# Edge rows, six walks, dense rows and the last hop in one part in place of four

## The chip, the cores and the metric

The kernel runs on one core of a Trainium2 chip. The metric is the device time of one execution in microseconds, from the core's own records; lower is better. The core has five engines that run side by side and wait for one another through semaphores: TensorE (PE, matrix products and transposes), VectorE (DVE), ScalarE (ACT), GpSimd (POOL, here the issuer of indirect gathers and scatters) and SyncE (SP, here the issuer of plain DMAs). Each engine executes its own instructions in order.

## The reference

Four graph layers act on 50000 nodes with 128 features and 12500 edges, sorted by destination. Each one adds to x what it makes of h = max(layernorm(x), 0):

```
x = x + gcn3(h)              # three weighted graph convolutions and a linear map
x = x + gin(h, edge_attr)    # mean over messages; W1, batch norm, relu, W2, batch norm, relu
x = x + walk6(h)             # six steps: h = h + relu(mean(h[src] into dst) @ Wh.T + bh)
x = x + gcn2(h)              # tanh(gcn(h, W1) + b1), then a second convolution's product W2
```

Only nodes that are the destination of an edge get anything from neighbours. The kernel computes the others, the great majority, as dense rows without a graph: for them the walks are a constant addition (relu of a bias, six times), and the last layer is two products with a tanh between them.

## The kernel before

Rows lie in groups of 512 (four tiles of 128 rows). There are DG = 98 dense groups (49 pairs), RG = 25 groups of "edge" rows (E: one row for the source of each edge) and 25 of "self" rows (S: one for the end of each run of edges with one destination). The edge list has NT = 98 tiles of 128, handled as 14 iterations of 4 + 3 tiles (halves b = 0 and 1). The parts are closed blocks with a barrier between them:

- First two layers' graph work and dense rows (0 to 1317 us), then the batch norms (1317 to 1917). The latter write y2_tab, turned group by group (`HI`, lines 1421 to 1438 for its loads and stores). The change touches only how self rows are loaded there.
- **Edge and self rows** (class `Late`, tag c, lines 1623 to 1726): 25 pairs. A pair loads y2 and x1, ScalarE applies the second batch norm and relu (L1594), PE turns it (L1601), DVE adds x1 (L1608), takes the moments (L206, L215), ScalarE the root (L221) and the normed rows (L252). Normed rows go to step_tab, what the third layer will be added to goes to x2_tab, with the constant r6 added for edge rows (L1720). The next load of x1 waits for this addition, since X1 has one buffer per half.
- **Walks and dense rows** (tag d, lines 1733 to 1962). Six walks of 14 iterations. In an iteration POOL gathers rows of step_tab (L287), PE turns them (L330 to L335), DVE sums along the edges by a scan (L344), PE multiplies by Wh (L355), DVE scales and adds the bias (L364) and updates RS (L1918), and SP stores RS to the other step_tab (L1889). POOL begins a walk only when all stores of the walk before have landed. Each gather buffer G[b] is used again once PE has turned it. `beside` orders the dense pairs between them by hand: one lone pair more than walks at the start, one lone pair before each walk, and one pair beside each two iterations ("a paired slot"): 7 lone pairs and 42 paired ones. In a pair DVE adds the rows three times: x2 (L1608), x3 (L1770), and the output rows of the pair before (L1796), whose products (L1818, L1825, L1831, L1833) PE does in the same slot, "late".
- **Third input** (tag p, lines 1974 to 2081): x2_tab and the walked rows are added for E and S rows, normed, and stored to last_tab (the fourth layer's input) and x3_s.
- **Last hop** (tag f, lines 2087 to 2183): 14 iterations: gather from last_tab, add RS (L315), turn, scan, product, affine, tanh (L2173), turn (L2157), copy (L2177), product (L2162), addition (L2141), and a scatter of the output rows by POOL (L2113), which stands between gathers: iteration i+1 is gathered before i is scattered.

## Time and profile before

| | |
|---|---|
| median of 3 runs | 3704.01 us (3700.06 to 3708.16) |
| the profiled execution | 3697.86 us |
| its span, first to last instruction | 3695.9 us |
| busy: PE, PE weight loads, DVE | 69%, 45%, 62% |
| busy: ACT, POOL | 54%, 40% |
| DMA | 549.48 MB, mean 149 GB/s |

The profile is one execution. Busy shares are averages over all parts. PEclk is the clock granted to TensorE as a share of 2.4 GHz (0.5 is 1.2 GHz). "Idle before" tells how long an engine stood before an instruction and what ended it.

### The profile page before, as it was taken

What the parts mean: (1) busy time and instruction counts of PE and PEld (TensorE: products, weight loads), DVE (VectorE), ACT (ScalarE), POOL (GpSimd) and SP (SyncE); (2) the same over time, 40 slices, a digit from 0 to 9 for tenths busy, and PEclk for the clock granted to TensorE, in tenths of its full rate; (3) what the DMA queues carried; (4) which work ended last, traced back from release to release, by engine and by line L of the source; (5) the groups of instructions that cost most, each with busy time, mean ns of one, the idle gap of its engine ahead of it and who ended that gap; (6) DMA issues with size and microseconds to landing.
All of it is one profiled execution on the core that took longest, in us unless ns stands there. A gap on an engine that the chain in (4) does not pass through costs nothing. (4 is left out here: it accounts for less than half of the span.)

```text
span 3695.9 us, 53510 instructions
## 1 busy us (share of the span) xinstructions
PE 2567.6 (69%) x11598; PEld 1680.0 (45%) x11598; DVE 2284.9 (62%) x8624; ACT 2000.0 (54%) x4312; POOL 1492.2 (40%) x1590
## 2 busy tenths in 40 slices
PE   5787677776566689999961116788888888840453
PEld 2455445544445544444431104555656565620343
DVE  6656777777775523333344327978888788878332
ACT  2788778565455535555544436665565656556110
POOL 6676762543325500000000003554555464635676
PEclk8999888897778889999985557888988898875666
DMA  4676554444545433333337664544444444349222
GB/s 102 197 203 192 146 153 147 141 140 144 146 136 160 144 109 135 135 136 136 136 135 234 215 206 139 160 151 144 145 146 152 141 150 130 118 145 294 68 73 62
DMA packets 548708, 549.48 MB, mean 149 GB/s; under 512 B 59898, under 2 KB 390891, under 8 KB 548400
## 3 DMA queue, kind: packets, MB, share of 16 engines
q1 hardware_dynamic: 490962, 441.21, 37.9%
q0 software_dynamic: 53264, 105.38, 10.3%
q10 hardware_dynamic: 4316, 1.13, 0.1%
q8 instruction: 51, 0.84, 0.1%
q14 instruction: 115, 0.93, 0.1%
HBM read 272.64 MB, written 279.69 MB: 149 GB/s over the span
## 5 line engine op out<-in xcount | busy, mean ns | idle before, releaser
L287 POOL DMA_INDIRECT h_G<-step_tab,row_i x588 | 565.5, 962 | 501.4 <-PE h_P L332 182.7
L287 POOL DMA_INDIRECT h_G<-msg_tab,row_i x294 | 283.0, 963 | 430.9 <-DVE h_M L307 181.5
L344 DVE TENSOR_TENSOR_SCAN h_T<-keep,h_T,h_P 128x384 f32<-128x384 f32 (+3 forms) x308 | 351.2, 1140 | 58.1 <-PE h_P L332 31.4
L808 PE MATMUL a_PA<-a_H,w 128*128 128x512 f32 x504 | 276.7, 680 | 94.3 <-ACT a_H L964 91.9
L252 ACT ACTIVATE d_NR<-d_X,d_ln_nm,d_ln_rs 128x128 f32<-128x128 f32 x784 | 311.7, 481 | 49.7 <-DVE d_ln_nm L235 49.7
L1513 DVE TENSOR_SCALAR b_Y<-b_BP,col 128x512 f32<-128x512 f32 x148 | 109.9, 742 | 354.1 <-PE b_BP L1467 354.1
L335 PE MATMUL h_P<-ident,h_M 128*128 128x128 f32 x490 | 100.5, 356 | 316.2 <-DVE h_M L315 249.6
L1467 PE MATMUL b_BP<-b_Z,w 128*128 128x512 f32 x592 | 266.3, 592 | 0.0
L1495 ACT ACTIVATE b_Z<-b_BQ,bn 128x512 f32<-128x512 f32 x148 | 115.0, 777 | 256.4 <-PE b_BQ L1459 256.0
L335 PEld LDWEIGHTS h_P<-ident,h_M 128*128 128x128 f32 x490 | 78.3, 186 | 356.1 <-DVE h_M L315 155.8
L1555 POOL TENSOR_TENSOR b_d<-b_d,neghalf 128x1 f32<-128x1 f32 x1 | 0.6, 568 | 592.1 <-DVE b_d L1546 592.1
L973 ACT ACTIVATE a_H<-a_PA,col 128x512 f32<-128x512 f32 x252 | 162.9, 669 | 87.9 <-PE a_PA L808 87.2
L252 ACT ACTIVATE a_HI<-a_X,a_ln_nm,a_ln_rs 128x128 f32<-128x128 f32 x490 | 200.9, 484 | 12.7 <-DVE a_ln_nm L235 12.7
L1601 PE MATMUL c_PT<-ident,c_ZT 128*128 128x128 f32 x200 | 49.6, 427 | 221.9 <-ACT c_ZT L1594 221.9
L1183 DVE TENSOR_TENSOR a_X<-a_XR,a_P 128x512 f32<-128x512 f32 x126 | 83.2, 670 | 186.9 <-PE a_P L830 185.2
L364 DVE SCALAR_TENSOR_TENSOR h_Z<-h_P,inv_cnt,rbh 128x128 f32<-128x128 f32 x588 | 162.2, 341 | 50.6 <-PE h_P L355 49.9
L808 PEld LDWEIGHTS a_PA<-a_H,w 128*128 128x128 f32 x504 | 97.0, 215 | 199.5 <-ACT a_H L964 121.6
L221 ACT ACTIVATE d_ln_sd<-d_ln_mv,lneps 128x8 f32<-128x8 f32 x98 | 29.2, 298 | 277.0 <-DVE d_ln_mv L215 277.0
L830 PE MATMUL a_P<-w3l,a_H 128*128 128x128 f32 x980 | 171.0, 327 | 0.0
L355 PEld LDWEIGHTS h_P<-wht,h_T 128*128 128x128 f32 x1176 | 147.1, 194 | 48.4 <-issue 37.7
L332 PE MATMUL h_P<-ident,h_G 128*128 128x128 f32 x980 | 167.0, 317 | 0.0
L252 ACT ACTIVATE a_NR<-a_XR,a_ln_nm,a_ln_rs 128x128 f32<-128x128 f32 x392 | 155.8, 484 | 12.7 <-DVE a_ln_nm L235 12.6
(343 smaller groups left out, 6549.2 us busy)
## 6 DMA issues: line engine op xcount, KB each, us to landing
b_HI<-hin_tab SPq DMA_DIRECT2D x148, 256.0 KB, 2.8
y_tab<-b_Y SPq DMA_DIRECT2D x148, 256.0 KB, 2.0
x_tab<-a_X SPq DMA_DIRECT2D x112, 256.0 KB
hin_tab<-a_HI SPq DMA_DIRECT2D x112, 256.0 KB
d_Y<-y_tab SPq DMA_DIRECT2D x98, 256.0 KB, 3.3
d_X<-x_tab SPq DMA_DIRECT2D x98, 256.0 KB
a_XR<-in_x SPq DMA_DIRECT2D x97, 256.0 KB, 4.1
out_rows<-d_O SPq DMA_DIRECT2D x97, 256.0 KB
```

The lines of the kernel that those rows point to most:

```text
L252: last = nc.scalar.activation(normed[:, k, :], rows[:, k, :], AF.Relu, scale=self.rs[:, c:c + 1], bias=self.nm[:, c:c + 1])
L287: pool.indirect_dma_start(out=G[b][:, j, :], out_offset=None, in_=self.table[:, :], in_offset=bass.IndirectOffsetOnAxis(ap=row_i[:, t + j: ...
L332: last = nc.tensor.matmul(PH[b][:, j * P:(j + 1) * P], rows[b][:, j, :], ident[:, :], start=False, stop=(j == nt - 1))
L335: last = nc.tensor.transpose(PH[b][:, j * P:(j + 1) * P], rows[b][:, j, :], ident[:, :])
L344: nc.vector.tensor_tensor_scan(T[b][:, 0:nt * P], keep[:, bass.ds(t * P, nt * P)], PH[b][:, 0:nt * P], T[1 - b][:, w - 1:w], ALU.mult, ALU ...
L355: last = nc.tensor.matmul(out_t, sums, self.W[:, :], start=True, stop=True)
L364: last = nc.vector.scalar_tensor_tensor(Z[b][:, j, :], PH[b][:, j * P:(j + 1) * P], self.scale[:, bass.ds(t + j, 1)], self.bias[:, :], ALU ...
L808: nc.tensor.matmul(PA[b][:, 0:nt * P], w[:, :], h[b][:, 0:nt, :].rearrange("p t d -> p (t d)"), start=True, stop=True).then_inc(done, 1)
L830: last = nc.tensor.matmul(P3[b][:, k * P:(k + 1) * P], H2[b][:, k, :], w3l[:, :], start=False, stop=(k == nt - 1))
L973: nc.scalar.activation(dst_h[b][:, 0:nt, :], PA[b][:, 0:nt * P], AF.Relu, bias=col[:, c:c + 1]).then_inc(done, 1)
L1467: last = nc.tensor.matmul(BP[b][:, :], w12[:, c, :], ZT[c][b][:, :], start=(c == 0), stop=(c == 1))
L1495: nc.scalar.activation(ZT[c][b][:, :], (BQ, BQ2)[c][b][:, :], AF.Relu, bias=bn1[:, 2 + c:3 + c], scale=bn1[:, c:c + 1]).then_inc(b_z[c], 1)
```

## The change

One block takes the place of the four behind the batch norms. Its slots are laid out in a list, and all loops are written out (no hardware loops).

- 25 slots of one pair each: self rows first (12 pairs and a half), then edge rows. Y, X1, X2, NR have two buffers per half. Edge rows get their third input at once: PE sums r6, X2 and the normed rows in PSUM, the second norm follows one slot later and goes to last_tab. Self rows stay in SBUF (XS), in place of x2_tab and x3_s.
- Walks: a lone dense pair ahead of walks 0, 1 and 2 alone. Seven paired slots in walks 0 to 4, six in walk 5, whose last slot has two iterations and no pair. Gathers alternate between the tiles G and M.
- In walk 5, each iteration also adds RS to XS, takes moments (`end_stats`), root (`end_rstd`) and norm (`end_norm`), stored to last_tab.
- Last hop: 14 slots of one iteration, with the last five dense pairs beside iterations 1, 3, 5, 7 and 9. All gathers come ahead of all scatters; the scatters wait for the dense stores.
- Output rows of a pair: PE adds X2 by a matmul with the identity, ScalarE copies the rows out (`rows_out`); L1796 goes.
- Batch-norm part: self groups are loaded with rows of one tile per partition (512 bytes each). free_d is bf16, and each iteration loads its share of it (`FR`).

```diff
-    free_d = dram("free_d", (1, EP))
+    free_d = dram("free_d", (1, EP), BF16)
-    x2_tab = dram("x2_tab", (2 * RR, D))
-    x3_s = dram("x3_s", (EP, D))
...
+                    if ends[b]:
+                        rows = hin_tab[bass.ds((2 * j + b) * GR, GR), :].rearrange("(k p) d -> p k d", p=P)
+                    else:
+                        rows = group_rows(hin_tab, 2 * j + b)
...
+    slots, left = [Slot3(j, ()) for j in range(D0)], collections.deque(range(D0, NJ))
+    ALONE3, LAST_PAIRS, TAIL_PAIRS = STEPS - 3, IT // 2 - 1, 5
+    for w in range(STEPS):
+        if w < ALONE3:
+            slots.append(Slot3(left.popleft(), ()))
+        for i in range(0, IT, 2):
+            with_pair = w < STEPS - 1 or i // 2 < LAST_PAIRS
+            slots.append(Slot3(left.popleft() if with_pair else None, (w * IT + i, w * IT + i + 1)))
+    for i in range(IT):
+        slots.append(Slot3(left.popleft() if i % 2 and left else None, (STEPS * IT + i,)))
...
+        @block.gpsimd
+        def _(pool):
+            def gather(i):
+                table = step_tab[i // IT % 2] if i < F0 else last_tab
+                for b in range(2):
+                    n, t, nt = hop_at(i, b)
+                    after(pool, wk_turn, n - 3)
...
+            for w in range(STEPS + 1):
+                for b in range(2):
+                    if 0 < w < STEPS:
+                        pool.wait_ge(wk_st[b], 16 * IT * w)
+                    if w == STEPS:
+                        pool.wait_ge(l_st[b], 16 * IT)
+                        pool.wait_ge(o_st[b], o_stores(D0, b))
+                for i in range(IT):
+                    gather(w * IT + i)
+            for b in range(2):
+                pool.wait_ge(o_st[b], o_stores(NJ, b))
+            for i in range(IT):
+                scatter(i)
...
+            def x3(j):
+                for b in range(2):
+                    if full(j, b):
+                        r = j % 2
+                        pe.wait_ge(ln1.normed, 2 * j + b + 1)
+                        nc.tensor.matmul(XB[r][b][:, :], ones3[:, :], split_r6[:, :], start=True, stop=False)
+                        if not is_d(j):
+                            nc.tensor.matmul(XB[r][b][:, :], ident[:, :], X2[r][b][:, :, :].rearrange("p t d -> p (t d)"), start=False, stop=False)
+                        nc.tensor.matmul(XB[r][b][:, :], ident[:, :], NR[r][b][:, :, :].rearrange("p t d -> p (t d)"), start=False,
+                                         stop=True).then_inc(x3_sum, 1)
...
+            def rows(j):
+                for b in range(2):
+                    n = 2 * (j - D0) + b
+                    pe.wait_ge(tanh_set, n + 1)
+                    pc_user[b] = (tanh_set, n + 1)
+                    nc.tensor.matmul(XB[j % 2][b][:, :], ident[:, :], X2[j % 2][b][:, :, :].rearrange("p t d -> p (t d)"), start=True, stop=False)
+                    nc.tensor.matmul(XB[j % 2][b][:, :], ones3[:, :], split_out[:, :], start=False, stop=False)
+                    for k in range(4):
+                        last = nc.tensor.matmul(XB[j % 2][b][:, k * P:(k + 1) * P], HT[b][:, k, :], w32[:, :], start=False, stop=(k == 3))
+                    last.then_inc(p2_set, 1)
...
+            for sl in slots:                                  # PE's order
+                j, its = sl.pair, sl.its
+                if j is not None and MIX < j <= D0:
+                    x3(j - 1)
+                if j is not None:
+                    turn(j)
+                for i in its[:1]:
+                    hop_turn(i)
+                if late is not None:
+                    turn2(late)
+                    prod(late)
+                for i in its[:1]:
+                    hop_prod(i)
+                if late is not None:
+                    rows(late)
+                for i in its[:1]:
+                    if i >= F0:
+                        end_turn(i - F0)
+                for i in its[1:]:
+                    hop_turn(i)
+                if j is not None and is_d(j):
+                    x3(j)
+                for i in its[:1]:
+                    if i >= F0:
+                        end_prod(i - F0)
+                for i in its[1:]:
+                    hop_prod(i)
...
+            for sl in slots:                                  # ScalarE's order
+                if late is not None:
+                    h(late)
+                if j is not None:
+                    ln1.act_std(act, j)
+                if j is not None and MIX < j <= D0:
+                    ln2.act_std(act, j - 1 - MIX)
+                for i in its[:1]:
+                    if LASTW < i < F0:
+                        pn.act_std(act, i - LASTW - 1)
+                        end_norm(i - LASTW - 1)
...
+                if late is not None:
+                    tanh(late)
+                for i in its[:1]:
+                    if i >= F0:
+                        end_tanh(i - F0)
+                if j is not None:
+                    z(j + 1)
+                    norm1(j)
+                    if j < D0 and j > MIX:
+                        norm2(j - 1)
...
+                if late is not None:
+                    rows_out(late)
...
+            for sl in slots:                                  # VectorE's order
...
+                if j is not None:
+                    x2(j)
+                    if MIX < j <= D0:
+                        stats2(j - 1)
+                for i in its[:1]:
+                    sums(i)
+                if j is not None:
+                    ln1.dve_rstd(dve, j)
+                    if MIX < j <= D0:
+                        rstd2(j - 1)
+                for i in its[:1]:
+                    if LASTW < i < F0:
+                        end_rstd(i - LASTW - 1)
+                    for b in range(2):
+                        affine(i, b)
+                    if i < F0:
+                        update(i)
+                    if LASTW <= i < F0:
+                        end_stats(i - LASTW)
+                for i in its[1:]:
+                    sums(i)
+                if j is not None and is_d(j):
+                    stats2(j)
+                for i in its[1:]:
+                    affine(i, 0)
+                    if i > LASTW:
+                        end_rstd(i - LASTW - 1)
+                if j is not None and is_d(j):
+                    rstd2(j)
+                for i in its[1:]:
+                    affine(i, 1)
+                    update(i)
+                    if i >= LASTW:
+                        end_stats(i - LASTW)
```

## Rows read from the trace of the kernel before

**Rows 1.** Windows by part: length, busy time (instructions) of PE, PEld, DVE, ACT, POOL, PEclk, DMA share, GB/s

```profile
1920.00:2191.00 271.00, 49.63 (x200) 38.94 (x200) 110.98 (x525) 120.16 (x275) 0.00 (x0) 0.50 0.65 216
2191.00:3285.00 1094.00, 892.70 (x4550) 613.26 (x4550) 864.34 (x2983) 647.44 (x1274) 566.15 (x589) 0.86 0.46 142
...
3424.00:3696.00 272.00, 126.91 (x588) 103.56 (x588) 92.67 (x182) 32.22 (x57) 192.52 (x196) 0.64 0.22 66
```

**Rows 2.** Windows: seven paired slots of walk 0, of walk 3, one lone pair

```profile
2256.00:2401.00 145.00, 114.12 (x596) 79.83 (x597) 132.74 (x450) 94.63 (x187) 84.81 (x90) 0.84 0.51 158
...
2767.00:2924.00 157.00, 134.68 (x712) 94.85 (x712) 133.10 (x448) 93.71 (x186) 86.37 (x90) 0.90 0.47 147
...
2751.00:2767.00 16.00, 14.76 (x60) 8.34 (x60) 9.33 (x43) 11.84 (x24) 7.84 (x9) 0.80 0.49 156
```

**Rows 3.** Timeline of a paired slot, walk 3: start, length, engine, line, [idle before]

```profile
2780.45 1.28 DVE L344 TENSOR_TENSOR_SCAN h_T<-keep,h_T,h_P 128x512 f32<-128x512 f32 x1 [0.90 <-PE h_P L332]
...
2795.43 1.01 DVE L344 TENSOR_TENSOR_SCAN h_T<-keep,h_T,h_P 128x384 f32<-128x384 f32 x1 [0.21 <-DVE h_T L344]
...
2797.37 0.39 PE L1831 MATMUL d_PC<-split_out,ones 3*128 3x512 bf16 x1
...
2799.65 1.32 DVE L1796 TENSOR_TENSOR d_O<-d_X,d_PC 128x512 f32<-128x512 f32 x2
...
2800.18 0.38 PE L330 MATMUL h_P<-freed,split_msg 9*128 x1
...
2801.99 1.28 DVE L344 TENSOR_TENSOR_SCAN h_T<-keep,h_T,h_P 128x512 f32<-128x512 f32 x1 [1.02 <-PE h_P L332]
```

**Rows 4.** Timeline, the same slot: identity matmul of a dense half, two passes

```profile
2803.03 1.12 PE L1810 MATMUL d_PC<-d_NR,ident 128*128 128x512 f32 x2
```

**Rows 5.** Timeline: POOL behind a walk, and the first gathers of the last hop

```profile
2754.81 0.95 POOL L287 DMA_INDIRECT h_G<-step_tab,row_i  x1 [16.79 <-DMA step_tab<-RS]
...
3426.43 1.02 POOL L287 DMA_INDIRECT h_G<-last_tab,row_i  x1 [5.62 <-POOLq L72]
...
3432.80 0.73 DVE L315 TENSOR_TENSOR h_M<-h_G,RS 128x512 f32<-128x512 f32 x1 [18.50 <-DMA h_G<-last_tab,row_i]
...
3436.57 0.60 DVE L315 TENSOR_TENSOR h_M<-h_G,RS 128x384 f32<-128x384 f32 x1 [3.04 <-DMA h_G<-last_tab,row_i]
```

**Rows 6.** Timeline: an edge pair, and the first input pass of the dense rows

```profile
1941.60 1.64 DVE L206 BATCH_NORM_STATS2 c_ln_st<-c_X 128x6 f32<-128x128 f32 x8
1941.78 3.18 ACT L252 ACTIVATE c_R<-c_X2r,c_ln_nm,c_ln_rs 128x128 f32<-128x128 f32 x8 [4.93 <-DVE c_ln_nm L235]
1943.41 0.64 DVE L215 BATCH_NORM_AGGREGATE c_ln_mv<-c_ln_st 128x2 f32<-128x6 f32 x8 [0.17 <-DVE c_ln_st L206]
1944.87 1.51 ACT L1594 ACTIVATE c_ZT<-c_Y,bn 128x512 f32<-128x512 f32 x2
1945.80 1.96 PE L1601 MATMUL c_PT<-ident,c_ZT 128*128 128x128 f32 x8 [7.75 <-ACT c_ZT L1594]
1949.05 0.69 DVE L1608 TENSOR_TENSOR c_X2r<-c_X,c_PT 128x512 f32<-128x512 f32 x1 [3.82 <-DMA c_X<-x_tab]
...
2221.48 0.81 ACT L1594 ACTIVATE d_ZT<-d_Y,bn 128x512 f32<-128x512 f32 x1 [33.71 <-DMA d_Y<-y_tab]
```

**Rows 7.** Timeline: PE behind the pause between walks 2 and 3

```profile
2751.20 1.12 PE L1818 MATMUL d_PC<-ident,d_NR 128*128 128x128 f32 x4 [3.79 <-ACT d_NR L252]
...
2753.65 3.62 PE L1825 MATMUL d_PC<-d_HT,w 128*128 128x512 f32 x4
```

**Rows 8.** Groups by line, 2000 to 3700: count | busy us, mean ns | idle before

```profile
L2113 POOL DMA_INDIRECT out_rows<-f_OR,end_i x98 | 97.1, 990 | 37.8 <-issue 29.3 <-DVE f_OR L2141 8.5
...
L1855 ACT ACT_TABLE_LOAD x49 | 62.9, 1283 | 0.9
```

**Rows 9.** Timeline: one iteration of the last hop, messages and output addition

```profile
3447.84 1.18 DVE L315 TENSOR_TENSOR h_M<-h_G,RS 128x512 f32<-128x512 f32 x2
...
3457.76 1.15 DVE L2141 TENSOR_TENSOR f_OR<-f_XR,f_P 128x512 f32<-128x512 f32 x2 [2.68 <-PE f_P L2162]
```

More of the change, by code:

```diff
@@ L1433, in _ @@
             load(1)
-            with sp.Fori(0, BPAIRS - 2) as j:
+            FIRST = (DG + RG) // 2
+            with sp.Fori(0, FIRST - 2) as j:
                 load(j + 2)
+                store(j)
+            load(FIRST, (False, True))
+            store(FIRST - 2)
+            with sp.Fori(FIRST - 1, BPAIRS - 2) as j:
+                load(j + 2, (True, True))
                 store(j)
@@ new lines, in group, with width, full, no2 @@
+    def group(j, b):
+        if j < MIX:
+            return 2 * j + b
+        if j == MIX:
+            return RG - 1
+        return 2 * (j - MIX - 1) + b if j < D0 else 2 * (j - D0) + b
+    def width(j, b):
+        return NT - 4 * (RG - 1) if j == MIX and b == 1 else 4
+    def full(j, b):
+        return kind(j, b) != "S"
+    def no2(j, b):
+        return max(j - MIX, 0) - (1 if b == 1 and j > MIX else 0)
+    def is_d(j):
+        return j >= D0
+    Slot3 = collections.namedtuple("Slot3", "pair its")
@@ new lines, in build, with hop_at @@
+    assert not left and slots[-1].pair is None and slots[-2].pair is None
+    LASTW, F0 = (STEPS - 1) * IT, STEPS * IT
+    def hop_at(i, b):
+        return 2 * i + b, first_tile(i % IT, b), SUB[b]
+    XS = sb(ctx, "XS", [P, NT, D])
+    FR = [sb(ctx, f"l_FR{u}", [3 * (STEPS - 1), sum(SUB) * P], BF16) for u in range(2)]
+    ring = lambda n: [[sb(ctx, f"l_{n}{r}{b}", [P, 4, D]) for b in range(2)] for r in range(2)]
+    Y, X1, X2, NR = ring("Y"), ring("X1"), ring("X2"), ring("NR")
+    HT, O = ([sb(ctx, f"l_{n}{b}", [P, 4, D]) for b in range(2)] for n in ("HT", "O"))
@@ L1655, in build, with r_stores, o_stores, rows2 @@
+    def r_stores(j, b):
+        return sum(32 for p in range(j) if p % 2 == j % 2 and kind(p, b) == "E")
+    def o_stores(j, b):
+        return 16 * no2(j, b)
+    def rows2(j, b):
+        return X2[j % 2][b] if full(j, b) else _Rows(XS, 4 * group(j, b))
     with nc.Block() as block:
@@ L1727, in build @@
-    end(ctx)
-    lctx = phase()
-    dl = Late(lctx, "d", True)
-    freed = sb(lctx, "freed", [3 * (STEPS - 1), EP], BF16)
-    rs_in, freed_in = sem("rs_in"), sem("freed_in")
-    HALF = IT // 2
-    def first(j):
-        return isinstance(j, int) and j == 0
-    def final(j):
-        return isinstance(j, int) and j == PAIRS - 1
-    def dl_load_next(sp, j):
-        if not (isinstance(j, int) and j == PAIRS - 1):
-            for b in range(2):
-                sp.wait_ge(dl.x2, 2 * j + b + 1)
-                dl.load(sp, j + 1, 0, b)
@@ L1827, in dl_pe_rows @@
-    def dl_pe_rows(pe, j):
-        for b in range(2):
-            q = 2 * j + b
-            pe.wait_ge(dl.tanh, q + 1)
-            nc.tensor.matmul(dl.PC[b][:, :], ones3[:, :], split_out[:, :], start=True, stop=False)
-            for k in range(4):
-                last = nc.tensor.matmul(dl.PC[b][:, k * P:(k + 1) * P], dl.HT[b][:, k, :], w32[:, :], start=False, stop=(k == 3))
-            last.then_inc(dl.p2, 1)
-    def dl_pe_end(pe, j):
-        dl_pe_turn2(pe, j)
-        dl_pe_prod(pe, j)
-        dl_pe_rows(pe, j)
@@ L2124, in _ @@
+            for b in range(2):
+                pool.wait_ge(o_st[b], o_stores(NJ, b))
+            for i in range(IT):
                 scatter(i)
@@ L2166, in _ @@
[L2166 to L2178 removed]
+                    q, r, n = 2 * j + b, j % 2, width(j, b)
@@ new lines, in affine @@
+            def affine(i, b):
+                n, t, nt = hop_at(i, b)
+                scale, bias = (inv_cnt, rbh) if i < F0 else (dinvu, rb31)
+                dve.wait_ge(wk_prod, n + 1)
+                if i <= F0:
+                    after(dve, wk_out, n - 1)
+                else:
+                    dve.wait_ge(f_prod, n - 2 * F0 - 1)
+                for k in range(nt):
+                    last = nc.vector.scalar_tensor_tensor(Z[b][:, k, :], PH[b][:, k * P:(k + 1) * P], scale[:, t + k:t + k + 1],
+                                                          bias[:, :], ALU.mult, ALU.add)
+                last.then_inc(wk_z, 1)
```

876 lines of the change are left out of this document (378 added, 498 removed).

## The prediction

> **What bounds the kernel now.** I read the busy times stage by stage first [rows 1]. The part behind the batch norms takes 1779 of the 3696 us: edge and self rows (271), walks with dense pairs (1094), the edge rows' third input (the 139 between 3285 and 3424), last hop (272). Then came the walks apart [rows 2]. Walk 3 has seven paired slots in 157 us, 22.4 each; the other walks from 1 to 5 span up to 159, so I use 22.6. Walk 0 gives 145/7 = 20.7, and a lone dense pair 16.0. Last came one paired slot in order of time [rows 3], because busy shares do not say which order matters: DVE is busy 85% of the walk windows, PE 86%.
>
> In that slot the loop is plain. DVE starts the scan of the second iteration at 2780.45 and is then occupied, with gaps of some tenths, until the scan of the next first iteration ends (2795.43 + 1.01 = 2796.44): 16.0 us. PE then finishes the product, starts the late pair's output rows at 2797.37, holds them until 2800.18, turns the gathered rows, and DVE's next scan starts at 2801.99, 5.55 us after the last. Together 21.54 us. The output addition of the late pair (L1796, 1.32 us) is done by 2800.97, and the scan behind it still waits 1.02 us for PE. So PE's work between two scans counts in full, and that DVE addition counts for nothing.
>
> **The change part by part.** I count profiled microseconds after minus before. The profiled run took 3697.86, 1.96 above its span, 6.15 below the median 3704.01; I add the sum of differences to the median.
>
> *Paired slots of walks 0 to 4.* The addition X2 + product moves from DVE into PSUM as a 128x512 fp32 matmul by the identity, once per half, and a ScalarE copy takes the rows out. DVE's 1.3 us was in the gap: gain 0. A 128x512 fp32 matmul is two passes, 1.12 us with its tail at full clock [rows 4]; I take 0.95 each, 1.9 per pair, between the two scans. The ring of two gather buffers removes PE's waits for gathers (0.9 us in most slots, ahead of the DVE-set point), which pays back part of any slow stretch but not of the loop above. So 21.54 + 1.9 = 23.45 for an undisturbed slot; I take 23.5 for the 28 slots of walks 1 to 4, against 22.6: +25. In walk 0, DVE's addition ended only as PE did, so a little comes back: 22.2 against 20.6, seven slots: +11. Bounds per slot: -1.3 (DVE is the bound and its addition is saved whole) to +1.9.
>
> *Lone pairs.* Seven before, three after. One costs 16.0 now [rows 2]; after, the same 1.9 longer, and the first also carries the last edge pair's second norm: 20 + 2 x 17.8 = 56 against 112: -56. But a lone pair covers the pause between walks: POOL gathers again only at 2754.81 [rows 5], 3.6 us after DVE has begun the lone pair [rows 2]. Where no lone pair stands, the first scans wait for that: four tiles need 3432.80 - 3426.43 = 6.4 us, all seven 10.1 [rows 5], so the second scan can start near 2754.8 + 10.1 + 1.3 = 2766.2, and end at 2767.2 instead of 2757.6 as DVE's order alone would have it. +9.6 at the walks 3, 4 and 5: +29.
>
> *Edge and self pairs (25 slots).* Before, each waits for its load, which is single buffered: DVE idles 3.8 us for it [rows 6], slots average 10.8. The rings of two take that wait away. Next late for a self pair: ScalarE's input pass 1.5, four transposes of its second half 1.1 (of 1.96 for eight), the addition 0.69, stats and aggregation 1.82 + 0.65, root 0.3: 6.1 us [rows 6]; DMA moves 1.5 MB in it, so I take 6.6. Twelve and the start: 5 + 79 us. An edge pair now gets its second norm here. The loop goes through all engines: first norm of half b0 1.6, on PE a small bf16 pass and four fp32 passes of 512 columns for each half (2.0 us at full clock, 3.9 at half) and the transposes (1.0 or 2.0), addition 0.7, two rounds of stats 2.5 each, roots and shifts 0.7, input pass 1.5, so that with the handovers I count 14.0 us with PE at full clock, 18.9 at half. PE idles over half of that. After 3.79 us of idleness its clock is at the lower level: four passes of 512 columns take 3.62 us [rows 7], 0.9 each, where two take 1.12 with their tail at the full one [rows 4]. I take 17 (PE slow in the first 6 us of its burst, as in that lone slot). 13 x 17 = 221. Together 305 us from the barrier to the first dense addition. Before it is 271 + 33 (ScalarE stands idle 33.71 us until 2221.48 behind the barrier, [rows 6]) = 306. So -1, with 13 x -3 to 13 x +2 around it.
>
> The Trainium skill, "TensorE: Matmul & The Clock Gate", section "HAM oscillation", says that a loop in which PE waits between bursts pays the cold clock once per burst. The trace agrees: 3.62 us behind the pause [rows 7]. By that rule alone, with every burst short, edge slots would be 18.9 and the term +24.
>
> *Third input.* x2_tab, x3_s and the stage that reads them go: -139. Its work for the self rows moves into walk 5: per iteration two additions, seven stats, seven aggregations (3.3 us on DVE) and a masked root (0.65), and seven norms on ScalarE (2.8 of the 3.18 for eight, [rows 6]).
>
> *Walk 5.* For a slot's first iteration DVE's 3.3 us fall into the gap before the second scan. ScalarE's do not: its norm of the previous iteration stands ahead of the tanh of the late pair, waits for DVE's masked root (7.15 us into the slot), and ends at 9.95; tanh's table 1.28 [rows 8] and b0 0.65 let PE begin the late rows at 11.9 instead of 7. PE has then idled 4 us and is slow for 6: rows and turn take 9 instead of 6.1; scan at 21. The second iteration's 3.3 + 0.65 on DVE are bare. Sum 21 + scan, third sum, stats, affine, root, update, end stats 14.5 = 35.5 us (32.5 with no slow clock). Six of these, one slot without a pair 27, and 7.3 us until its norms are stored and POOL gathers: 247. Before: 7 x 22.6 + 12 of drain (the two products behind the last update) = 170. +77.
>
> *Last hop.* Before POOL alternates 98 gathers and 98 scatters, 1.26 us apart ([rows 5], three more tiles in 3.8) and 1.29 (0.99 and 0.30 of issue, [rows 8]): 250 of 272 us. After, all gathers come first, hidden behind dense pairs, and the scatters last: 98 x 1.29 = 126 us in which no other engine has work. They start when the 14th gather is out, and that needs the turn of iteration 11. Iterations without a pair take 11.1 us from messages to output ([rows 9], 3447.84 to 3458.91), and are no longer overlapped. Per pair, two slots: one with the pair 21 (full clock) to 24, the next with its late rows 15 to 20; I take 40 for both. 7 + 3 (first gathers) + 11.6 + 5 x 40 + 3.5 + 8.8 + 126.4 + 2.5 = 363: +91. Bounds 36 and 44: +71 to +111.
>
> The self rows' loads of 512 bytes in the batch-norm part lie under a PE that runs without a pause; nought. The bf16 free flags save a small copy; nought.
>
> Sum: 25 + 11 - 56 + 29 - 1 - 139 + 77 + 91 = +37. 3704 + 37 = **3741 us**.
>
> **The rivals.**
> 1. *The clock stays up* (faster). PE has more work per slot and loses its waits for gathers; if the granted clock stays at the full level in edge slots, walk 5 and last hop: 13 x -3, 6 x -3, 5 x -4, 28 x -0.3, and the self rows near 6.1 (-6): -91, so 37 - 91 = -54: 3650. For it: the walks hold 0.90. Against: 0.64 in the last hop and 0.50 with the edge rows, where bursts are short [rows 1, 2]. It decides the sign once 37 of these 91 us come back. 17%.
> 2. *DVE is the bound of paired slots* (faster). Then each loses 1.3 instead of gaining 0.9 to 1.6: 28 x -2.2, 7 x -2.9, lone ones 3 x -2: -88: 3653. For it: DVE's 85%. Against: the 1.02 us wait in [rows 3]. 6%.
> 3. *Slow stretches everywhere* (slower than forecast). PE at the low clock behind each wait for the affine rows: paired slots 24.2 (+20), edge 18.9 (+25), last hop 44 a pair (+20), walk 5 37 (+9): 3815. 22%.
> 4. *It nets out*: the terms of +77 and +91 are each some 17 too high: 3707. 13%.
>
> **How the numbers follow.** Forecast 42%, the rivals as given. About 0.2%, 7 us, is what a measurement tells from no change. Faster: rivals 1 and 2, 0.23, and little of 4: 0.25. Same: most of 4, 0.12. Slower: 0.63. The forecast's own range is 3715 to 3770; with the others cut at one in ten on either side 3665 to 3805.
>
> **What would show it.** Scan to scan in a paired slot of walks 1 to 4: 23.5 us with the identity matmuls right behind the tanh and DVE idle some 3 us before the second scan; under 22 means rival 2. Edge slots 17 us apart and a granted clock between the levels; 14 means rival 1. DVE idle some 8 us at the start of walks 3, 4 and 5. In walk 5 ScalarE's norm of RS ahead of each tanh, slots of 35. At the end 126 us of scatters alone, starting some 235 us after the first gather of the last hop. If compute of the last hop ends early and POOL starts scattering before that, or the slots of walk 5 stay under 30, the prediction fails there.

## The result, and the profile after

The change makes the kernel slightly slower: median 3711.11 us (3701.69 to 3721.35, 20 runs) against 3697.44 us (3688.70 to 3708.16, 20 runs) for the kernel before, ratio 1.0037, 95% interval 1.0029 to 1.0046. Two later jobs gave 1.0036 and 1.0032. That is +14 us where +37 was forecast. The profiled execution spans 3708.4 us, 12.5 more than before.

Windows of the kernel after, columns as in [rows 1]: twelve self slots, twelve edge slots, walk 0, the second lone pair, walks 1 and 3, four paired slots of walk 5, and the last hop ahead of its scatters and from them on.

```profile
1921.70:1995.70 74.00, 23.62 (x98) 18.83 (x97) 47.42 (x241) 54.87 (x126) 0.00 (x0) 0.50 0.84 254
2006.60:2212.40 205.80, 97.84 (x218) 38.70 (x217) 75.97 (x457) 92.87 (x236) 0.00 (x0) 0.69 0.42 150
2230.70:2383.40 152.70, 126.34 (x623) 80.16 (x623) 123.69 (x435) 101.61 (x201) 81.68 (x86) 0.90 0.47 146
2383.40:2400.90 17.50, 15.40 (x64) 8.56 (x64) 7.83 (x41) 12.44 (x24) 10.74 (x12) 0.90 0.59 183
2400.90:2563.80 162.90, 142.59 (x740) 94.09 (x740) 124.52 (x435) 101.53 (x201) 83.51 (x87) 0.95 0.44 138
2744.30:2919.60 175.30, 146.59 (x756) 98.23 (x756) 124.56 (x436) 99.79 (x197) 94.25 (x98) 0.91 0.45 138
3134.70:3271.90 137.20, 99.80 (x432) 61.42 (x432) 98.67 (x401) 80.90 (x177) 58.36 (x60) 0.81 0.33 103
...
3338.00:3571.50 233.50, 172.19 (x766) 115.64 (x767) 115.18 (x355) 108.61 (x196) 93.24 (x99) 0.76 0.17 52
3571.50:3708.40 136.90, 15.66 (x92) 11.86 (x91) 13.73 (x27) 4.33 (x8) 95.88 (x98) 0.57 0.12 38
```

The seven slots of walk 3 take 175.3 us where before they and the lone pair ahead of them took 157 + 16 [rows 2]. In the last 136.9 us POOL issues the 98 scatters (95.9 us busy); the other engines end their last iterations in the first 23 us of it (PE 15.7 us busy, DVE 13.7, ScalarE 4.3) and then stand idle. The steady slot of walks 1 to 4, timeline of DVE and PE (as [rows 3]):

```profile
2688.37 2.38 DVE L2118 TENSOR_TENSOR_SCAN h_T<-keep,h_T,h_P 128x512 f32<-128x512 bf16 x2 [3.71 <-PE h_P L1865]
...
2701.95 2.35 DVE L2118 TENSOR_TENSOR_SCAN h_T<-keep,h_T,h_P 128x512 f32<-128x512 bf16 x2
...
2711.28 2.39 DVE L2118 TENSOR_TENSOR_SCAN h_T<-keep,h_T,h_P 128x512 f32<-128x512 bf16 x2 [3.78 <-PE h_P L1865]
...
2705.14 1.02 PE L1844 MATMUL l_XB<-l_X,ident 128*128 128x512 f32 x2
...
2709.76 0.38 PE L1863 MATMUL h_P<-l_FR,split_msg 6*128 6x512 bf16 x1
```

Scan to scan is 22.91 us, and DVE stands 3.78 us for PE before the second scan (some 3 forecast). PE's output rows now last 4.62 us (2705.14 to 2709.76) where they took 2.81 [rows 3]: the identity passes cost 1.81.

From boundary to boundary of the two traces, after minus before, forecast in brackets: self and edge pairs from the barrier to the first dense addition -11.2 (-1); lone pairs 18.3 + 17.5 + 17.4 = 53.2 against 112.9, -59.7 (-56); walk 0 +8.2 (+11); walks 1 to 4 with two of the boundaries +41.8 (+25 +19); walk 5 with its boundary, to POOL's first gather of the last hop, +74.1 (+77 +10); third input -141.4 (-139); last hop +100.7 (+91). Sum +12.5, the difference of the spans.

### The profile page after: what moved, and what is told of

It is laid out like the page before. It is cut to its first block and busy times, and to the rows that moved or that the text cites. A ratio compares the mean times of both kernels' runs of the same rounds, so it can differ in the third digit from the quotient of the medians.

```text
span 3708.4 us, 48145 instructions
## 1 busy us (share of the span) xinstructions
PE 2722.3 (73%) x11947; PEld 1703.4 (46%) x11947; DVE 2178.1 (59%) x8443; ACT 2055.6 (55%) x4419; POOL 1429.5 (39%) x1505
## 5 line engine op out<-in xcount | busy, mean ns | idle before, releaser
L1762 POOL DMA_INDIRECT h_G<-step_tab,row_i x294 | 289.5, 985 | 542.5 <-DMA step_tab<-l_NR 300.1
L1762 POOL DMA_INDIRECT h_M<-step_tab,row_i x294 | 280.0, 953 | 274.3 <-PE h_P L1865 170.1
L2118 DVE TENSOR_TENSOR_SCAN h_T<-keep,h_T,h_P 128x512 f32<-128x512 bf16 x196 | 223.4, 1140 | 213.0 <-PE h_P L1865 180.5
L219 ACT ACTIVATE l_ln_sd<-l_ln_mv,lneps 128x8 f32<-128x8 f32 (+1 forms) x136 | 40.9, 301 | 479.5 <-DVE l_ln_mv L2090 313.0
L250 ACT ACTIVATE l_NR<-l_X,l_ln_nm,l_ln_rs 128x128 f32<-128x128 f32 x492 | 195.2, 482 | 0.0
L1181 DVE TENSOR_TENSOR a_X<-a_XR,a_P 128x512 f32<-128x512 f32 x126 | 83.3, 671 | 190.1 <-PE a_P L828 188.4
L1963 ACT ACTIVATE l_NR<-l_X,l_ln_nm,l_ln_rs 128x128 f32<-128x128 f32 x392 | 156.0, 480 | 39.5 <-DVE l_ln_nm L2101 39.5
L2130 DVE SCALAR_TENSOR_TENSOR h_Z<-h_P,inv_cnt,rbh 128x128 f32<-128x128 f32 x588 | 162.2, 342 | 17.5 <-PE h_P L1876 17.4
L1876 PE MATMUL h_P<-wht,h_T 128*128 128x128 f32 x1176 | 154.6, 281 | 11.3 <-DVE h_T L2118 11.2
L1821 PE MATMUL l_XB<-l_NR,ident 128*128 128x512 f32 x246 | 158.5, 731 | 0.0
```

The lines of the kernel that those rows point to most:

```text
L250: last = nc.scalar.activation(normed[:, k, :], rows[:, k, :], AF.Relu, scale=self.rs[:, c:c + 1], bias=self.nm[:, c:c + 1])
L1762: pool.indirect_dma_start(out=GR_[i % 2][b][:, k, :], out_offset=None, in_=table[:, :], in_offset=bass.IndirectOffsetOnAxis(ap=row_i[:, t ...
L1821: nc.tensor.matmul(XB[r][b][:, :], ident[:, :], NR[r][b][:, :, :].rearrange("p t d -> p (t d)"), start=False, stop=True).then_inc(x3_sum, 1)
L1876: last = nc.tensor.matmul(PH[b][:, k * P:(k + 1) * P], T[b][:, k * P:(k + 1) * P], (wht if i < F0 else w31)[:, :], start=True, stop=True)
L1963: last = nc.scalar.activation(to[:, k, :], rows, AF.Relu, scale=ln2.rs[:, c:c + 1], bias=ln2.nm[:, c:c + 1])
L2118: nc.vector.tensor_tensor_scan(T[b][:, 0:nt * P], keep[:, t * P:(t + nt) * P], PH[b][:, 0:nt * P], T[1 - b][:, w - 1:w], ALU.mult, ALU.add ...
```

## The experiments

Eighteen runs were made, in five jobs: twelve kernels, four of them twice, and the changed kernel itself twice. In the second and the fourth job (e4, e8, e5, e7; c1, c4, e7b, e4b) everything took longer: the part up to the start of the new block, the same in all kernels after, ended at 2209 to 2274 us in place of 1916 to 1929, and the kernel before took 4181 and 4130 us. From these two jobs I use comparisons inside a job alone. I took their transfers for slow, and the expectations below say so, but the profiles do not bear it out. Windows of that common part, the kernel after and e7b (fourth job):

```profile
100.00:1917.00 1817.00, 1442.59 (x6066) 897.82 (x6064) 1042.74 (x4067) 1089.23 (x2424) 604.12 (x632) 0.90 0.49 147
```

```profile
100.00:2214.00 2114.00, 1521.23 (x6088) 947.84 (x6087) 1050.33 (x4104) 1095.18 (x2430) 610.97 (x638) 0.84 0.42 128
```

The DMA engines were busy as long in both (0.49 x 1817 and 0.42 x 2114 us, 890 and 888) and moved about the same bytes in a longer time. What the slow job adds are waits for which the profile names no releaser: before L1181, for example, DVE stood 204 us in such waits ("remote" 113.6, "issue" 90.0), against 1.7 in the kernel after. What held the engines there is not known. I call these two the slow jobs.

**e1: the output addition back on DVE.** PE's identity matmul goes, and DVE adds X2 from SBUF to the product in PSUM behind the first affine and update.

```diff
-  nc.tensor.matmul(XB[j % 2][b], ident, X2[j % 2][b], start=True, stop=False)
-  (ScalarE) activation(O[b], XB[j % 2][b], AF.Copy)
+  (VectorE) tensor_tensor(O[b], X2[j % 2][b], XB[j % 2][b], ALU.add)
```

> The changed kernel with one part undone: the output rows of a dense pair are added by VectorE again, behind the update of the slot's first iteration, and the identity matmul of X2 and ScalarE's copy are gone. Theory A (the prediction's: what PE does between the scan of a first iteration and the scan of the second counts in full, and VectorE's addition lies in the wait for it): a paired slot of walks 1 to 4 falls from 22.9 us by the two identity matmuls, 0.95 each, to 21.1; in walk 5 from 34.3 to some 31 (PE is at its low clock there, two passes take up to 2.1); walk 0, bound by both, 21.1 to 20.3. Over 28 + 7 + 6 slots, three lone ones and five pairs of the last hop some 75 us, 3636 by the clock of the 3711. Theory B (the slot is bound by VectorE's own work): VectorE gets 1.3 us more per slot and the slot grows to 24. Theory C (nothing in it, the cost was only ScalarE's): 22.9 stays.

Measured 3632.29 us, ratio 0.9822 (0.9805 to 0.9839), 79 below the kernel after. Steady slots are 21.18 us each (21.1 expected). DVE's timeline in one of them:

```profile
2632.80 1.42 DVE L2094 TENSOR_TENSOR l_O<-l_X,l_XB 128x512 f32<-128x512 f32 x2
2634.94 2.38 DVE L2122 TENSOR_TENSOR_SCAN h_T<-keep,h_T,h_P 128x512 f32<-128x512 bf16 x2 [0.72 <-PE h_P L1864]
```

DVE does the addition and then still waits 0.72 us for PE: it was free there, as the forecast took it to be, and PE's passes were not. 22.91 - 21.18 = 1.73 a slot, close to the 1.81 by which the passes had lengthened PE's rows. (ScalarE's copy left with them; e1 does not part the two.) This one edit is the difference between a change that costs 14 us and one that saves 63.

**e2: the late pair ahead of a walk's first gathers** on PE, in the slots where walks 3, 4 and 5 begin.

```diff
+  if early: turn2(late); prod(late)
   for i in its[:1]: hop_turn(i)
-  if late is not None: turn2(late); prod(late)
+  if late is not None and not early: turn2(late); prod(late)
```

> The changed kernel with TensorE's order changed in three slots, the first of walks 3, 4 and 5, which have no lone pair ahead of them: the late pair's transposes and first product come before the transposes of the walk's first gathered rows. Theory A (the pause costs more than predicted because TensorE, waiting for the gather, has the late pair's work queued behind it): the first slot of walks 3 and 4 falls from 37.5 to some 33, that of walk 5 from 40.4 to 36, and the kernel by 12 to 15 us to 3697. Theory B (the extra comes from gathers or stores landing later than predicted): no change of the three slots beyond 0.5 us.

Measured 3700.63 us, 1.0019 (1.0007 to 1.0031), 10.5 below after. The start of walk 3 in the kernel after, POOL, PE and DVE:

```profile
2747.68 0.95 POOL L1762 DMA_INDIRECT h_G<-step_tab,row_i  x1 [27.70 <-DMA step_tab<-RS]
...
2753.94 0.60 PE L1863 MATMUL h_P<-l_FR,split_msg 9*128 9x512 bf16 x1 [13.49 <-DMA h_G<-step_tab,row_i]
...
2759.52 1.92 PE L1830 MATMUL l_PC<-ident,l_NR 128*128 128x128 f32 x8
2761.27 2.98 PE L1837 MATMUL l_PC<-l_HT,w 128*128 128x512 f32 x4
2764.09 1.72 PE L1876 MATMUL h_P<-wht,h_T 128*128 128x128 f32 x14
...
2771.79 2.39 DVE L2118 TENSOR_TENSOR_SCAN h_T<-keep,h_T,h_P 128x512 f32<-128x512 bf16 x2 [3.64 <-PE h_P L1865]
```

And in e2:

```profile
2742.46 3.36 PE L1837 MATMUL l_PC<-l_HT,w 128*128 128x512 f32 x4
2749.60 0.60 PE L1863 MATMUL h_P<-l_FR,split_msg 9*128 9x512 bf16 x1 [3.78 <-DMA h_G<-step_tab,row_i]
...
2755.25 3.19 PE L1876 MATMUL h_P<-wht,h_T 128*128 128x128 f32 x14
```

PE waited 13.49 us for the gather with the late pair's work queued behind it, and only then did that work (4.6 us) ahead of the first product. Moved into the wait, it brings the first slots of walks 3, 4, 5 from 37.5, 37.1, 40.4 to 34.8, 35.0, 38.9: 6.3 us, half of what was expected. The first product starts 4.5 us sooner in its slot, but then takes 3.19 us in place of 1.72. The other 4.2 us are not of the edit: in the profiled executions 1.2 lie ahead of the new block and 3.0 in the edge part (287.7 us for 290.7), which the edit leaves alone, and a second execution of the unaltered kernel (r1_after) takes 287.4 there.

**e3: ScalarE norms RS behind the late tanh.** `end_norm` of a slot's first iteration moves from ahead of `tanh(late)` to behind the pair's norms.

```diff
   pn.act_std(act, i - LASTW - 1)
-  end_norm(i - LASTW - 1)
   if late is not None: tanh(late)
   ... norm1(j) ...
+  end_norm(i - LASTW - 1)
```

> The changed kernel with ScalarE's norm of the walked rows (end_norm of a slot's first iteration, walk 5 alone) moved from ahead of the late pair's tanh to behind its own first norm of the dense pair. Theory A (that norm, with its wait for VectorE's masked root, is what makes walk 5's slots long): a slot of walk 5 falls from 34.3 by the 2.8 of the norm and 1 to 2 of wait and of TensorE's slow clock, to 29 to 31; six slots, 20 to 30 us, 3686. Theory B (VectorE's stats are the bound of these slots: its work sums to 27.5 with the gaps that remain): less than 2 us a slot, 3700 or more.

Measured 3673.28 us, 0.9942 (0.9924 to 0.9961): -38, where 20 to 30 were expected. Walk 5's slots fall from 34.3 to 26.6. One slot of it in the kernel after:

```profile
3210.24 2.80 ACT L250 ACTIVATE RS<-XS,p_ln_nm,p_ln_rs 128x128 f32<-128x128 f32 x7 [2.58 <-DVE p_ln_nm L233]
3213.06 1.28 ACT L1978 ACT_TABLE_LOAD   x1
...
3215.09 2.08 PE L1844 MATMUL l_XB<-l_X,ident 128*128 128x512 f32 x2 [4.71 <-ACT l_HT L1978]
...
3223.98 2.38 DVE L2118 TENSOR_TENSOR_SCAN h_T<-keep,h_T,h_P 128x512 f32<-128x512 bf16 x2 [7.70 <-PE h_P L1865]
```

And in e3:

```profile
3185.63 1.28 ACT L1978 ACT_TABLE_LOAD   x1
3186.92 1.26 ACT L1978 ACTIVATE l_HT<-l_PC,col 128x512 f32<-128x512 f32 x2
...
3188.35 1.02 PE L1844 MATMUL l_XB<-l_X,ident 128*128 128x512 f32 x2
...
3194.49 2.38 DVE L2120 TENSOR_TENSOR_SCAN h_T<-keep,h_T,h_P 128x512 f32<-128x512 bf16 x2 [0.26 <-PE h_P L1865]
```

The late rows on PE begin 6.9 us after the slot's start (3181.47) in place of 11.6 (3203.51), and without the pause of 4.71 us PE does them at the upper clock: an identity pair of passes takes 1.02 where it took 2.08. DVE's idle time before the second scan falls from 7.70 to 0.26, which is what the slot gains.

**e6: the kernel before with its walk loops written out**, nothing else.

```diff
-  with eng.Fori(0, HALF - 1) as k:
+  for k in range(HALF - 1):
```

> The kernel before with one edit: the hardware loops over the paired slots of the walks are written out, all else is as it was. Theory A (half a microsecond of the difference between the predicted 23.45 and the measured 22.9 us of an undisturbed slot is what loop registers and computed addresses cost at the handovers between VectorE and TensorE): slots of walks 1 to 5 fall from 22.6 on average by 0.3 to 0.5, and the kernel by 12 to 18 us, to 3682. Theory B (the 0.5 comes from something else, such as the second gather buffer): no change within 3 us.

Measured 3690.89 us, 0.9986 (0.9971 to 1.0001): not told from no change by the times, and less than the 12 to 18 us that theory A asked of the kernel. Windows of walks 1 to 4 with their lone pairs, kernel before and e6:

```profile
2416.60:3115.20 698.60, 602.73 (x3088) 415.90 (x3088) 570.75 (x1960) 423.53 (x833) 377.92 (x393) 0.88 0.47 146
```

```profile
2421.10:3110.20 689.10, 596.10 (x3088) 414.74 (x3088) 569.17 (x1962) 423.02 (x832) 375.99 (x393) 0.89 0.47 149
```

9.5 us in 28 slots, 0.3 each, from one execution of either. So of the 1.4 by which e1's slots (21.18) are shorter than those of before (22.6), loops give 0.3. That the rest comes of PE's missing waits for gathers is argued, not shown.

**e5: a busy PE in the edge slots.** Sixteen more matmuls per edge pair, into a PSUM tile that nobody reads then.

```diff
+  if MIX < j < D0:
+      for r in range(16):
+          nc.tensor.matmul(PC[r % 2][:, 0:2 * D], w31, w11, start=True, stop=True)
```

> The changed kernel with 16 more matmuls (128x256, results overwritten) on PE behind the transposes of each edge pair, in the time in which PE stands idle. It asks whether the 17.1 of an edge slot hold a share of low clock. Theory A (PE's passes at the low clock cost 3 of the 17.1, as the prediction put it): slots of about 14 to 15, granted clock near 1.0 there, 12 slots 25 to 35 less. Rival B (ScalarE and DVE round the loop set it, or the added work itself is in the way): slots within 0.5 of 17.1 or longer.

Windows of eleven edge slots, e5, and e7 as its base in the same job (its one gather buffer plays no part in edge slots):

```profile
2361.90:2528.40 166.50, 143.46 (x553) 94.69 (x552) 69.73 (x419) 86.46 (x220) 0.00 (x0) 0.95 0.48 171
```

```profile
2371.10:2558.70 187.60, 88.56 (x200) 35.03 (x199) 69.67 (x418) 86.40 (x220) 0.00 (x0) 0.70 0.43 152
```

With 353 more passes (16 matmuls of two passes in each slot) the stretch is 21 us shorter: slots of 17.06 become 14.38 (six) or 15.98 (five), and the granted clock is 0.95 in place of 0.70. The total, 4135.24 us, ratio 0.9879 (0.9840 to 0.9917), is 22 above e7's 4113.31: walks 3, 4 and 5 began with slots of 48.9, 49.0 and 52.0 us where e7's were 38.4, 37.4 and 42.9. RS's stores are not the cause, since POOL's first gather of walk 3 comes 3.4 us after the slot's start in both. In e5 DVE then stands 11.5 us before the affine rows (L2133), against 4.5, and 4.7 before a reciprocal (L230), against 1.8, for reasons that the profile does not name. So the edit's worth in a job like the first was not measured.

**e7 and e7b: one gather buffer.**

```diff
-  GR_ = [G, M]
+  GR_ = [G, G]
...
-  after(pool, wk_turn, n - 3)
+  after(pool, wk_turn, n - 1)
```

> The changed kernel with one gather buffer per half in place of two, so that a gather waits for the turn of the iteration before it. It asks what the second buffer gives back in the paired slots. Theory A: the slots of walks 1 to 4, an even 22.9 now, spread between 22 and 24.5 again and grow by 0.5 to 1 (PE waits for gathers at the head of a slot, some tenths of a us to 1.2 of waiting): total +15 to +30. Rival B (PE waits were hidden in any case): within 5.

> The changed kernel with one gather buffer per half. Theory A: slots of walks 1 to 4 grow from an even 22.9 to 23.4 or more, the size the forecast gave them; total +15 to +30 (3725 to 3740). Theory B (the second buffer hides nothing in an undisturbed slot): slots 22.9, total within 5, and the forecast's 23.5 was high for another reason: the pause around PE's section was counted too long.

4113.31 us (0.9831, 0.9796 to 0.9865) and 4056.17 us (0.9832, 0.9801 to 0.9862), both in slow jobs. Walk 1's six slots behind its first, e7b, and e4b with two buffers in the same job:

```profile
2731.30:2876.20 144.90, 128.63 (x640) 86.29 (x640) 107.72 (x373) 85.73 (x169) 73.42 (x77) 0.89 0.44 139
```

```profile
2734.50:2875.70 141.20, 126.84 (x640) 85.51 (x639) 107.75 (x374) 85.18 (x168) 66.50 (x70) 0.91 0.45 140
```

0.6 us a slot for the second buffer, in a slow job (in walk 1 both kernels place their pairs alike). In the other jobs it was not measured. Ratios near 0.983 say little of the buffer: in the slow jobs every kernel with the new block gained on the one before, and the changed kernel itself never ran in such a job (r2_after met an ordinary one).

**e4 and e4b: pairs back where they were; e8 and e8b: none in the last hop, POOL in turn.** All four also put the late pair ahead on PE where the last hop starts, as e2 does for the walks, and issue the last store of normed rows sooner.

```diff
-  ALONE3, LAST_PAIRS, TAIL_PAIRS = STEPS - 3, IT // 2 - 1, 5
+  e4: STEPS, IT // 2, 1     e8: two lone pairs ahead of walk 0, one ahead of the others, IT // 2, 0
...
   e8 only:
-  for i in range(IT): gather(F0 + i)
-  for i in range(IT): scatter(i)
+  gather(F0); gather(F0 + 1); scatter(0)
+  for i in range(1, IT): gather(F0 + i + 1) (to IT - 1); scatter(i)
```

> The changed kernel with its dense pairs placed nearly as before: a lone pair ahead of every walk (six), a pair beside all seven slots of walk 5, one pair in the last hop in place of five; nothing else differs, scatters still follow all gathers. Theory A (the terms as read from the two traces): three more lone pairs +52 (17.5 each), the first slots of walks 3 to 5 fall from 37, 37 and 40 to about 24 (-43), one more pair in walk 5 +9 (34.3 for 25.3), four pairs less in the last hop -75 (41 for two iterations with a pair, some 22 without): -57, about 3654. Rival B (pairs beside the last hop are free, since gathers and scatters by POOL bound it as they did before): the last hop stays within 15 of its 370, and the sum is about 3700 or more.

> The changed kernel with no pair in the last hop (two lone pairs ahead of walk 0, one ahead of each other walk, seven beside walk 5) and with POOL taking the gathers and scatters of the last hop in turn, as before. Theory A: the last hop takes the 270 that it took before instead of 370 (-100); four more lone pairs +70, first slots -43, walk 5 +9: -64, about 3647. Rival B (alternating makes gathers late, because one iteration now has norms and stores ahead of it): the last hop stays above 330, about 3710.

> The changed kernel with six lone pairs, seven pairs in walk 5 and one in the last hop; scatters behind all gathers. On the slow chip its last hop took 354 from the first gather, there against some 382 with five pairs. Theory A (the pairs ride in idle time, the scatters behind the gathers are what costs): last hop 330 to 350 here, 60 to 75 more than e8b's 275 and 20 to 40 less than the changed kernel's 370; total 3685 to 3705. Theory B (pairs cost 19 each beyond an iteration's own length): last hop about 295, total about 3650.

> The same placement as e8: no pair in the last hop, seven lone pairs, gathers and scatters of the last hop in turn. On the slow chip the last hop without pairs took 341 from its first gather where 270 were expected, and POOL waited 82 us for DVE's output rows. Theory A (expected first, 270 for the last hop): 64 below the changed kernel. Theory B (the last hop is longer because one iteration's work no longer overlaps the next one's; its five pairs ride in time that is idle anyhow): last hop about 340 against 370, so -30 +70 -43 +9: within 15 of the changed kernel.

e8b, in an ordinary job: 3665.24 us, 0.9921 (0.9902 to 0.9940), 44 below the changed kernel (r1_after, 3709.58, same job), expected 64; by spans 56.6. Its last hop takes 275.4 from the first gather, where the changed kernel's took 370.7: theory A. The same kernel's 341 in e8 was the slow job's. e8 was 4121.99 (0.9843, 0.9812 to 0.9874). e4 and e4b, both in slow jobs: 4119.13 (0.9836, 0.9805 to 0.9866) and 4067.39 (0.9855, 0.9819 to 0.9891). e4b's last hop took 349.7 where e7b's with five pairs took 386.7, so four pairs less are worth 37 there, 9 each; in the other slow job e4 took 354.0 against 386.2 (e7) and 402.1 (e5), so this is rough. c1 below, no pair and in turn, took 323.4 in e4b's job: 26 less. What e4 gives in an ordinary job, where 57 us were expected, was not measured.

**e9, c3, c4: two iterations overlapped in the last hop.** DVE adds and scans iteration i+1, and PE turns it, ahead of iteration i's end. c3 is e9 with e1, e3 and e2's order. c4 has one edit more:

```diff
-  gather(F0 + i + 1) ahead of scatter(i)
+  gather(F0 + i + 2) ahead of scatter(i)
```

> e8 with one thing more: in the last hop DVE adds and scans iteration i+1, and PE turns it, ahead of the tanh, turn and product of iteration i, so that two iterations overlap as they did in the kernel before. Theory B above: POOL's 196 gathers and scatters at 1.27 become the bound again, last hop 255 to 275, 70 less than e8b. Theory A (alternation alone was enough, or the time goes to something else): within 10 of e8b.

> All that gained, together: e9's placement and overlap, the output addition back on DVE (e1, -77), the norms of RS behind the affine half of the slot (e3, -38; one slot of walk 5 more has a pair now, so somewhat more), the late pair first where a walk or the last hop starts (e2; here only at the last hop, since lone pairs stand before the walks). Theory A (the gains add): -77 -42 and e9's -85 from the changed kernel's 3710: about 3505, 0.948 of before. Rival B (they share the same idle time, half of the smaller ones is lost): about 3560.

e9: 3759.28 us, 1.0174 (1.0155 to 1.0192), 94 above e8b, against both theories. c3: 3661.05 us, 0.9901 (0.9872 to 0.9930), 156 above theory A and 101 above rival B. POOL's groups in the last hop (count | busy, mean ns | idle before), e8b, e9 and c4b:

```profile
L1770 POOL DMA_INDIRECT out_rows<-XS,end_i x98 | 99.5, 1015 | 38.4 <-issue 29.3 <-DVE XS L2164 9.1
```

```profile
L1770 POOL DMA_INDIRECT out_rows<-XS,end_i x98 | 96.5, 985 | 139.8 <-DVE XS L2167 112.3 <-issue 27.5
```

```profile
L1770 POOL DMA_INDIRECT out_rows<-XS,end_i x98 | 98.5, 1005 | 29.9 <-issue 29.6 <-DVE XS L2173 0.3
```

And e9's order in time, POOL and DVE:

```profile
3419.39 0.95 POOL L1762 DMA_INDIRECT h_G<-last_tab,row_i  x1 [0.30 <-issue]
...
3421.89 0.56 DVE L2119 TENSOR_TENSOR h_G<-h_G,RS 128x384 f32<-128x384 f32 x1 [3.03 <-DMA h_G<-last_tab,row_i]
...
3427.59 0.69 DVE L2167 TENSOR_TENSOR XS<-XS,l_PC 128x512 f32<-128x512 f32 x1 [2.85 <-PE l_PC L1900]
...
3429.11 1.01 POOL L1770 DMA_INDIRECT out_rows<-XS,end_i  x1 [8.76 <-DVE XS L2167]
```

POOL gathers for i+1 and then waits to scatter i; DVE's output rows of i now stand behind its work on i+1, which waits for that very gather. So POOL idles ahead of each iteration's scatters, some 8.7 us a time, 112 us in all. I had moved the work on one queue and not asked what the other queue's order relied on.

> e8's placement and its gathers and scatters in turn, with e1 (addition on DVE), e3 (norms of RS later on ScalarE) and e2's order at the last hop; it is c3 without the overlap that lengthened e9. In c3 the last hop began at 3288 from the start; e8b's takes 275 from there. Theory A (c3's 3661 holds all of e9's error): about 3565, 0.965 of before. Theory B (the overlap was not the cause there): near 3660.

> c3_best with one change in POOL's order: two iterations are gathered before the first is scattered, and so on. In e9 POOL stood idle 112 us before scatters, because DVE's output rows of iteration i stood behind its addition for i+1, which waits for the gather that POOL issued last. Theory A (that ring of waits is what e9 lost): the last hop falls from 373 to POOL's own 196 x 1.28 = 251 and some 10 to 20 around it, about 3555, 5 to 15 below c1. Rival B (the overlapped order itself is slow, ScalarE's 213 us of waiting for PE's turns): it stays over 3600.

> The changed kernel unaltered, as the base for the three others on the same chip. The job before this one landed on a chip where the kernel before takes 4181 us, and had no such base: there the kernel with one gather buffer was at 0.983 of before. Theory A (on a chip like the first, before at 3697): 1.0037 of before, as measured. Theory B (should the chip be the slow one): 0.98 or below, since the slow chip's stores and loads cost the four old blocks with their barriers more than the one new block.

> The changed kernel unaltered. If this job finds fast transfers (before near 3697): 1.0037 of before again. If it finds slow ones (before over 4100): Theory A (slow transfers cost the four old blocks more, and the buffer adds little) 0.980 to 0.986; Theory B (the second gather buffer does harm under slow transfers, or the old kernel is not hit harder) 0.995 or more.

> All gains together, with the overlapped last hop and two iterations gathered ahead. Under slow transfers it was 0.963 of before. With fast ones, Theory A (gains of e1, e3 and e8 add, and the last hop is at POOL's own 251 plus 10 to 20): 3288 + 265 = about 3553, 0.961 of before. Theory B (the last hop stays as long as in c3, 373, its cause another): about 3660, 0.99. Under slow transfers again: 0.963, within 0.004.

c1 (c3 without the overlap) and c4, in a slow job: 3993.55 (0.9670, 0.9636 to 0.9703) and 3974.64 us (0.9632, 0.9603 to 0.9662), ratios of 0.965 and about 0.961 expected; c4 is 19 below c1. r1_after 3709.58 (1.0036, 1.0020 to 1.0053) and r2_after 3712.14 (1.0032, 1.0020 to 1.0043) repeat the result. c4b, in an ordinary job: **3555.64 us, 0.9612 (0.9597 to 0.9628)**, expected 3553; it beats both kernels, by 145 and 156 us. Its window of the last hop, and the changed kernel's:

```profile
3283.40:3545.20 261.80, 141.00 (x634) 113.50 (x634) 93.87 (x184) 31.21 (x56) 194.28 (x196) 0.63 0.15 46
```

```profile
3338.20:3708.40 370.20, 187.84 (x856) 127.50 (x856) 128.91 (x382) 112.94 (x204) 189.12 (x196) 0.69 0.15 47
```

## Why the prediction was right or wrong

The sign, the order of events and the signs of all terms came as forecast. The size did not: +14 for +37. The terms are large and opposed (some 200 us each way), and three of them were mis-sized: self and edge pairs (-11 for -1), walk 5 with its boundary (+74 for +87) and the last hop (+101 for +91). That the sum came within 24 us is in part luck, since the last hop's error stands against the others.

- **Self and edge pairs, 10 too high.** Half is the self slots: 6.17 each against 6.6, in twelve. The other half is the mixed slot, 10.9 us, which I counted among thirteen at 17; the twelve others took 17.1. Clock 0.69 and 17.1 are what "PE slow in the first part of its burst" asked for, and in e5, at 0.95, six of eleven slots take 14.4, near the 14.0 counted for a full clock. The 18.9 a slot that I had estimated by the rule of the Trainium skill ("TensorE: Matmul & The Clock Gate", section "HAM oscillation") taken alone was too high: the measured 17.1 decides.
- **Walk 5 with its boundary, 12.5 too high, the largest miss.** Scan at 20.5 (21 forecast), ScalarE's norm ended at 9.5 (9.95), late rows at 11.6 (11.9), the rest 13.8 (14.5): each step right, each a little dear, 34.3 for 35.5 in five slots. The slot without a pair and the drain took 2.2 less, the boundary with its first slot 4.7 less. e3 confirms the cause, ScalarE's queue order, and that I saw it as a price of the change without drawing its worth: 38 us.
- **Walks 1 to 4: 2 too high, but from two errors that nearly cancel, which is luck.** Here a step failed in its mechanism and not in size alone. The loop in [rows 3] is 21.54; I added 1.9 and took 23.5, it is 22.91: the passes cost 1.81, the turn is scanned 0.29 sooner, the hand to the rows 0.09, DVE's part 0.07. Then 28 slots give -17. Against it stood the boundary, 14.6 and 14.2 in place of 9.6: I followed POOL and DVE, not PE's order, where the late pair stands behind the turn that waits for the gather. e2 gives back 2.7 and 2.2 of these 5.0 and 4.6; the rest is not explained. And the first slots behind a lone pair are 25.1 and 25.6, not 23.5.
- **Lone pairs -4, walk 0 -3**: a lone pair with the passes takes 17.4 to 17.5 (17.8 forecast), the first one 18.3 (20), a slot of walk 0 21.8 on average (22.2).
- **Last hop, 10 too low.** First scatter at 233.3 behind the first gather (234 forecast), pairs 41.0 (40), scatters 125.5 (126.4). The end behind the last scatter took 11.5 us (3696.9 to 3708.4), not 2.5. The kernel before has one of 9.6 (3686.3 to 3695.9), within its 269.5, for which I had 272.
- **Rival 1** (full clock) is refuted for edge slots (0.69), walk 5 (0.81) and the last hop (0.76), windows above; its self slots near 6.1 came, and in the walks, at 0.90 to 0.95, its paired slots came and went further (22.91, where it asked for 23.2). **Rival 2** (DVE the bound) by the 3.78 us that DVE waits, and by e1. **Rival 3** did not come: the slots are even. **Rival 4**, 3707, was the nearest number, by another way than it said: its two terms did not come in 17 lower each, the one was 12.5 lower and the other 10 higher.

Open stay what held the engines in the slow jobs, the half of the longer boundary that e2 does not give back, and, for ordinary jobs, the worth of the second buffer, of e5's busy PE and of e4's placement.

## What to carry to other kernels

Before moving an operation to another engine, look at who waits for whom at its place: here DVE waited 1 us behind an addition that looked like load on an 85% busy engine, and moving it to the engine that was waited for cost 79 us. When a wait for a far event (a gather behind a pause) stands in an in-order queue, put finished work ahead of it; when work is advanced on one engine, check which other queue's order leaned on the old place. Where opposed terms of a hundred us are summed, read each slot and tail to tenths, since 0.6 in 28 slots outweighs the answer.

## What the runs showed of the hardware that I had not expected

- Useless matmuls made a stretch shorter: 353 more passes in eleven edge slots, 187.6 to 166.5 us, granted clock 0.70 to 0.95.
- The same kernel on the same chip can differ by 12% from job to job: 3695.6 and 4130.3 us for the kernel before. The DMA engines' busy time did not grow with it (888 for 890 us in the common part); the engines' waits without a named releaser did. Ratios between kernels shift with it: one and the same kernel was at 0.9921 (e8b) and at 0.9843 (e8) of the kernel before.
- The tail behind the last scatter is 11.5 us, though each scatter lands 2.1 to 2.3 us after its issue. Most of it is POOL's drain at the end of the block: 8.9 us in the kernel after, 7.5 before (first and second line), 5.4 in c4b.

```profile
L1656 POOLq DRAIN  x1: 8877/8877/8877, 3698.4 to 3698.4; - x1
```

```profile
L2097 POOLq DRAIN  x1: 7485/7485/7485, 3687.8 to 3687.8; - x1
```
